# Flamingo attention with routed experts: key projection moved from 256-column to 512-column matmuls with dimensions on the partitions, rotary halves crossed by ScalarE, values of two head pairs in one product

## What is computed

```
lat = layer_norm(_layernorm(x));  ctx = layer_norm(context)
q = (lat @ Wq)                       # 16 heads of 64, "pairs" of heads are 128 columns
k, v = split(ctx @ Wkv)
k = apply_rope(k, cos, sin)          # x1*cos - x2*sin | x2*cos + x1*sin, halves of 32 in each head
attn = softmax(clip(q k^T / 8, -11, 11))
x = x + tanh(g_xattn) * ((attn @ v) @ Wo + bo)
x = x + tanh(g_ffn) * (routed experts + shared expert)(_layernorm(x))
```

## Time and profile before

| | |
|---|---|
| median of 3 runs | 2723.12 us |
| profiled execution, its own time | 2726.36 us |
| its span, first to last instruction | 2724.6 us |
| TensorE busy | 2419.1 us, 89% |
| VectorE busy | 2125.0 us, 78% |
| GpSimd busy | 1989.4 us, 73% |
| ScalarE busy | 1163.4 us, 43% |
| mean granted TensorE clock | 0.96 of full speed |

### The profile page before, as it was taken

One profiled execution on the slowest core, in us unless ns is written; L12 is line 12 of the kernel. 1 busy time (PEld: TensorE's weight loads), 2 busy tenths in 40 slices (PEclk: granted clock), 3 DMA queues, 4 the chain that ended last, 5 costly groups with the idle time before them and its releaser, 6 DMA issues. The chain is left out here.

```text
span 2724.6 us, 47912 instructions
## 1 busy us (share of the span) xinstructions
PE 2419.1 (89%) x13494; PEld 1471.9 (54%) x13494; DVE 2125.0 (78%) x4785; ACT 1163.4 (43%) x2652; POOL 1989.4 (73%) x2550
## 2 busy tenths in 40 slices
PE   2999999999989998999999899989996986998991
PEld 1555555555555555555555555545553655987780
DVE  4877788887888787878778787888787666688884
ACT  2444444444344444443444344344442332676660
POOL 2777677689868886988698789868885731067776
PEclk9999999999989998999899999999997997999995
DMA  8334334111111211111121111111111516799994
GB/s 302 136 123 147 109 109 148 47 45 49 49 46 48 69 47 45 49 51 54 40 67 50 48 45 49 49 46 50 68 47 53 198 38 239 238 309 318 328 324 148
DMA packets 157368, 301.61 MB, mean 111 GB/s; under 512 B 20066, under 2 KB 95778, under 8 KB 156834
## 3 DMA queue, kind: packets, MB, share of 16 engines
q1 hardware_dynamic: 128994, 230.95, 25.0%
q0 software_dynamic: 24576, 67.14, 7.5%
q10 hardware_dynamic: 3520, 0.27, 0.1%
HBM read 170.37 MB, written 127.93 MB: 109 GB/s over the span
## 5 line engine op out<-in xcount | busy, mean ns | idle before, releaser
L925 ACT ACTIVATE e<-scores 128x1024 f32<-128x1024 f32 x520 | 533.9, 1027 | 920.0 <-PE scores L807 897.3
L1020 POOL TENSOR_SCALAR e<-e 128x1024 f32<-128x1024 f32 x520 | 613.7, 1180 | 50.4 <-ACT e L925 6.9
L1200 DVE TENSOR_TENSOR e_sum<-e_sum,e 128x1024 f32<-128x1024 f32 x391 | 582.1, 1489 | 5.7 <-POOL e L1020 5.5
L847 PE MATMUL ps_o<-e,v 128*64 128x512 f32 x2088 | 567.5, 622 | 0.4 <-POOL e L1020 0.4
L807 PE MATMUL scores<-q_t,k_t 64*128 64x512 f32 x3120 | 503.8, 427 | 28.9 <-DVE affine L1143 13.9
L819 PE MATMUL ps_kv<-w,ctx_t 128*128 128x256 f32 x3072 | 507.7, 302 | 11.9 <-DVE ctx_t L1150 8.5
L819 PEld LDWEIGHTS ps_kv<-w,ctx_t 128*128 128x128 f32 x3072 | 401.4, 191 | 202.0 <-issue 173.5
L807 PEld LDWEIGHTS scores<-q_t,k_t 64*128 64x128 f32 x3120 | 257.5, 185 | 391.3 <-issue 251.5
L1728 POOL DMA_INDIRECT room<-results_in_blocks,index x256 | 247.0, 965 | 210.4 <-DMA results_in_blocks<-room 130.5
L1010 POOL TENSOR_TENSOR k_rot<-rope_c,rope_s 128x64 f32<-128x64 f32 x513 | 323.2, 630 | 68.4 <-PE ps_kt L837 23.0
L1014 POOL TENSOR_TENSOR k_rot<-rope_c,rope_s 128x64 f32<-128x64 f32 x513 | 203.6, 397 | 195.3 <-ACT e L925 193.0
(11 more groups left out here) (287 smaller groups left out, 3553.3 us busy)
## 6 DMA issues: line engine op xcount, KB each, us to landing
w<-w_pairs SPq DMA_DIRECT2D x65, 768.0 KB, 4.5
rows_in_blocks<-room SPq DMA_DIRECT2D x16, 2560.0 KB, 11.3
x_nat<-rows_in_blocks SPq DMA_DIRECT2D x160, 256.0 KB
results_in_blocks<-room SPq DMA_DIRECT2D x80, 512.0 KB
wo<-in_L_xattn_Wo SPq DMA_DIRECT2D x66, 128.0 KB, 4.5
x_nat<-in_ctx SPq DMA_DIRECT2D x64, 128.0 KB, 4.3
down_all<-in_L_ffn_down_w SPq DMA_DIRECT2D x16, 512.0 KB, 8.6
w_pairs<-w_split SPq DMA_DIRECT2D x8, 768.0 KB, 7.1
```

What stands on the lines that cost most here:

```text
L847: mm = pe.matmul(ps_o[hh * DH:(hh + 1) * DH, :], v[:, buf, tile, hh * DH:(hh + 1) * DH], e[:, tile % 4, hh * N:(hh + 1) * N], start=(tile ...
L925: act.activation(e[:, c % 4], scores[:, c % 2], ACT.Exp, scale=SCALE).then_inc(s_exp, 1)
L1020: pool.tensor_scalar(e[:, c % 4], e[:, c % 4], EXP_HI, EXP_LO, ALU.min, ALU.max).then_inc(s_clip, 1)
L1200: dve.tensor_tensor(total, e[:, 0] if c == 2 else total, e[:, tile % 4], ALU.add).then_inc(s_sum, 1)
```

## The change

Keys and values are projected apart. A "double" is two pairs. In the even pair of a double, each step projects the values of both pairs for 128 context rows (256 moving columns of `wv`, into `ps_v`); in the odd pair there is no such product. The keys of a pair are projected in two halves, at c = 0 and c = 4: the key columns of `wqk` are stationary and 512 context rows of `ctx_t` move, so that the result in `ps_k` has dimensions on the partitions and is not transposed. Queries move from c = 0 to c = 2 and use `ps_k` too.

The rotation of a half is a chain: ScalarE copies the four groups of 32 partitions crossed into `k_sw` (c = 0 and 4), VectorE multiplies `ps_k` by cos and `k_sw` by signed sin (c = 1 and 5), GpSimd adds the two (c = 2 and 6), ScalarE makes the high part (c = 3 and 7), VectorE the rest (c = 4 and 7). The product `o_n` is done in two halves (c = 3 before the clip, c = 4 behind it). In `boundary` the context comes before the latents. Slots and gates of the routing go to DRAM (`store_all`) and are read back in `finish_routing`, which frees SBUF for the cos and sin tables, now 128 x 1024, made in `setup` with 16 transposes.

```diff
-                    pe.wait_ge(s_rope, g * 8 + c + 1)
+                if project and jj == 0:
...
+                    pe.wait_ge(s_v, 1 + g // 2 * 8 + c)
...
-                            mm = pe.matmul(ps_kv[:, 0:2 * P], ctx_t[:, a, cc, c * P:(c + 1) * P],
-                                           w[:, jj, bb, cc, 1:3].rearrange("p t m -> p (t m)"),
+                            mm = pe.matmul(ps_v[:, 0:2 * P], ctx_t[:, a, cc, c * P:(c + 1) * P], wv[:, bb, cc],
...
+                if project and c in (0, 4):
...
+                    else:
+                        pe.wait_ge(s_qlo, 2 + g)
+                    pe.wait_ge(s_cos, 1 + g * 2 + half)
...
+                            mm = pe.matmul(ps_k[:], wqk[:, jj, bb, cc, 1], ctx_t[:, a, cc, half * N:(half + 1) * N],
...
-                if project or (attend and c < 2):
-                    pe.wait_ge(s_klo, 1 + g * 8 + c)
-                    pe.wait_ge(s_rot, 2 + g * 8 + c)
-                    pe.transpose(ps_kt[:, 0:P], k_rot[:, c % 2].rearrange("p h d -> p (h d)"), pers.ident[:]
-                                 ).then_inc(s_kt, 1)
...
+                if project and c in (0, 4):
+                    half = c // 4
+                    act.wait_ge(s_k, g * 2 + half + 1)
+                    act.wait_ge(s_turned, 1 + g * 2 + half)
+                    for q in range(4):
+                        to, of = slice(q * 32, (q + 1) * 32), slice((q ^ 1) * 32, (q ^ 1) * 32 + 32)
+                        st = act.activation(k_sw[to], ps_k[of], ACT.Copy)
+                    st.then_inc(s_swapped, 1)
...
+                if project and c in (3, 7):
+                    half = c // 4
+                    act.wait_ge(s_turned, 1 + g * 2 + half + 1)
+                    act.activation(k_t[:, jj, 0, half * N:(half + 1) * N], k_c[:], ACT.Copy).then_inc(s_khi, 1)
...
+                if project and c in (2, 6):
+                    half = c // 4
+                    pool.wait_ge(s_sin, g * 2 + half + 1)
+                    pool.tensor_tensor(k_c[:], k_c[:], k_sw[:], ALU.add).then_inc(s_turned, 1)
+                if c == 3:
+                    pool.wait_ge(s_rec, g * 2 + 1)
+                    pool.wait_ge(s_oraw, g + 1)
+                    pool.tensor_tensor(o_n[:, 0:D], o_raw[:, 0:D], r_den[:, 0:D], ALU.mult).then_inc(s_on, 1)
...
+                if project and c == 3:
+                    dve.wait_ge(s_qe, g + 1)
+                    dve.tensor_tensor(q_t[:, jj, 1], ps_k[:], f32(q_t[:, jj, 0]), ALU.subtract).then_inc(s_qlo, 1)
+                if project and c in (1, 5):
...
+                    dve.wait_ge(s_swapped, g * 2 + half + 1)
+                    dve.tensor_tensor(k_c[:], ps_k[:], rope.cos[:, tokens], ALU.mult).then_inc(s_cos, 1)
+                    dve.tensor_tensor(k_sw[:], k_sw[:], rope.sin[:, tokens], ALU.mult).then_inc(s_sin, 1)
```

More of the change, by code:

```diff
@@ L154, in part, with more_part, shaped @@
         assert self.taken_up <= ROOM
+        return self.shaped(a, shape)
+    def more_part(self, start, *shape):
+        n = math.prod(shape)
+        assert start + n <= MORE
+        return self.shaped(self.more[:, start:start + n], shape)
+    @staticmethod
+    def shaped(a, shape):
         if len(shape) == 2:
@@ L703, in batch @@
                 for p in range(PAIRS):
-                    pair(b, p // 2, p % 2, p)
+                    pair(b, p // 2, p % 4, p)
             if boundary:
                 boundary(0)
-            with eng.Fori(0, PAIRS // 2) as i:
-                for jj in range(2):
-                    pair(0, i, jj, None)
+            with eng.Fori(0, DOUBLES // 2) as i:
+                for m in range(4):
+                    pair(0, i * 2 + m // 2, m, None)
             batch(1)
@@ L1259, in _ @@
             sp.dma_start(sdn[:], ins["shared_down_w"].rearrange("(k p) n -> p k n", p=P)).then_inc(shared_loaded, 16)
+            for whole, dram in ((router.slot_all, slots_dram), (router.gate_all, gates_dram)):
+                sp.dma_start(whole[:, 0:last * GT].rearrange("p (g t) e -> p g (t e)", t=GT),
+                             dram.rearrange("g p n -> p g n")).then_inc(all_loaded, 16)
             for e in range(0, E_R, 8):
@@ L1537, in experts @@
         xs = pers.x_nat[:, 0:XR]
-        land = kept.part(TOP_K, D)
-        y = kept.part(YR, D)
+        land = kept.more_part(0, TOP_K, D)
+        y = kept.more_part(TOP_K * D, YR, D)
         x_t = pers.x_nat[:, XR:XR + 4]
@@ L1751, in program @@
         router = Router(nc, ctx, pers, kept)
-        setup(nc, pers, ins, w_dram)
-        attention(nc, pers, ins, w_dram, xs_dram, router)
+        with ExitStack() as tables:
+            rope = Rope(nc, tables)
+            setup(nc, pers, rope, ins, wqk_dram, wv_dram)
+            attention(nc, pers, rope, ins, wqk_dram, wv_dram, xs_dram, slots_dram, gates_dram, router)
+        kept.more = ctx.enter_context(nc.sbuf_tensor("more", [P, MORE], F32))
         up = ctx.enter_context(nc.sbuf_tensor("up_all", [P, E_R, D], F32))
-        finish_routing(nc, pers, ins, kept, router, up, xs_dram, table_dram)
+        finish_routing(nc, pers, ins, kept, router, up, xs_dram, table_dram, slots_dram, gates_dram)
         experts(nc, pers, ins, out, kept, up, xs_dram, y_dram)
```

347 lines of the change are left out of this document (197 added, 150 removed).

## The result

The changed kernel takes 2643.62 us (median of 4 runs, 2637.58 to 2649.16) against 2722.78 us for the kernel before on the same chip: a ratio of 0.9706, 95% interval 0.9682 to 0.973. It is faster by 79 us, where 155 were forecast.

A forecast was written before the change was run, and what follows sets the result against it. TensorE was taken to bound attention, with VectorE nearly as full in two pairs of eight. Terms: -102.8 - 32 - 61.2 + 38.5 + 2 = -155.5 us, from 2726.4 to 2570.9, as median 2568; range 2530 to 2635.

The forecast's parts named there:

- (a): TensorE in attention: 514 transposes of 0.20 us are gone, saving 102.8 us in full.
- (b): TensorE's projection: 6.06 us a pair instead of 6.56, through groups of 512 columns, saving 32 us.
- (c): TensorE's time by pair after the change: 29.3 us for an even pair, 22.7 for an odd one.
- the distances between queries: Sign in the timeline: queries of even pairs 29 to 32 us from the next, odd ones near 23.
- (d): TensorE's waits in attention: 23.4 us for `k_rot`, 30 for `o_n` and 7.8 for `ctx_t` go, together 61.2.
- (e): VectorE late in pairs 5 and 7: 5.5 us in each of 7 routed batches, +38.5 us, bounds 0 and 60.
- (f): ScalarE's crossed copies in the key chain: 0.59 us each, room for 1.5, so nothing charged.
- (g): GpSimd in attention: loses 16 rotary operations, gets two additions and `o_n` in halves, and gets easier.
- (h): Around attention: setup copies and transposes, routing read back in `finish_routing`, `wv` load: +2 us, bounds 0 and 8.
- pairs 1 and 3 over 24 us: Sign that the forecast of VectorE's lateness, +38.5 us, would be wrong.
- a granted clock below 1.00 in an odd pair: Sign that the whole forecast would be wrong; the clock fell before only around boundaries (0.89).
- Rival B: VectorE bounds all odd pairs through collisions with GpSimd, 42 us and some 35 more, about 2645 us; chance 20%.

The follow-up runs named there:

- f5: Kernel before plus three VectorE operations (128 x 512, two SBUF inputs) at c = 4 of pairs 5 and 7 of routed batches: attention ends 20.4 us later.
- f6: Kernel before plus three VectorE operations (128 x 512, two SBUF inputs) at c = 4 of pairs 2 and 4 of routed batches: attention ends 33.7 us later.
- e4: Changed kernel with one uncrossed ScalarE copy of 128 partitions for four crossed ones of 32: attention ends at 2024.3 us against 2018.6 for the changed kernel run again.
- e5: Changed kernel with the rotary additions moved from GpSimd to VectorE, right behind its products: 17 us gained against the changed kernel run again.
- e1: Changed kernel with GpSimd's clip cut to 8 of 1024 columns of each exponential: attention ends 97 us earlier.
- b1: Kernel before with GpSimd's clip cut to 8 of 1024 columns of each exponential: attention ends 90 us earlier.
- e3: Changed kernel with the rest of the queries ahead of the second reciprocal on VectorE: wait for it 44.4 to 15.0 us, no time gained.
- e7: Changed kernel with three pieces of VectorE's routing moved from odd pairs to the end of even ones: 25 us gained, 22 against the changed kernel run again.
- e2: Changed kernel with VectorE's reciprocals on half of the columns only: attention ends 25 us earlier, time by the ratio some 2628 us.
- f1: Changed kernel plus three VectorE operations (128 x 512, two SBUF inputs) at c = 4 of pairs 5 and 7 of routed batches: costs 28 us.
- f4: Changed kernel plus three VectorE operations (128 x 512, two SBUF inputs) at c = 4 of all eight pairs of the first batch: costs 7.9 us.

## Why the prediction was wrong

The direction was right, and the size was missed by the 8.6 us by which 2643.62 lies over the range, and by 76 us from the number. By the steps of the prediction:

- (a), 102.8 us: right. The transposes took 0.20 us each, and they are gone.
- (b), 32 us, is **the term that was mis-sized: it saved nothing**. With no transpose behind it the projection's distance is 0.91 in five of the eight steps of an even pair, and 0.82 only where keys or queries follow. A key group took 1.47 to 1.60, on average 1.53, where 1.39 was taken from queries that had a transpose behind them. So a pair has 4 x 0.87 + 2 x 1.53 = 6.56 us, which is what 8 x 0.82 took before. The queries, in no term, went from 1.39 to 1.53 as well, 9 us in 64 pairs. Where exactly the loss is booked is a choice: put the other way, a transpose that goes saves 0.11 us where the product moves up to the projection (0.82 + 0.20 less 0.91). Together (a) and (b) brought 3.2 us in two plain pairs, 104 in 32 doubles, and not 134.8.
  The formula that the prediction set aside stands in the Trainium skill (TensorE: Matmul & The Clock Gate, section Back-to-back issue gap) for a matmul by itself; the page says that in a stream with weight loads it is too low for few columns and too high for 512. The traces agree with the first, 137 to 152 ns for 256 columns against an estimate of 109 by the formula, and not with the second, 232 to 267 for 512 against an estimate of 216. That the formula would have had (b) at nothing, as it came, is luck.
- (c), an even pair of 29.3 and an odd one of 22.7 us: near. The stretches above hold one of the eight projections on the other side of the cut, 0.9 us, so 28.77 and 23.77 are 29.7 and 22.9, 0.5 more in two pairs; the pair of 28.09 from which it was worked out has 0.15 us of idle time in it. (The marker given for it, the distances between queries, was not right: queries at c = 2 cut the doubles elsewhere.)
- (d), 61.2: 60.5 measured.
- (e), 38.5, is **the step that failed**: the new waits for VectorE are some 96 us, beyond its upper bound of 60. VectorE's load was forecast well in pair 5 (25.9 us, 25.80 measured), and so were the waits for the queries in pairs 5 and 7 (half of 3.2 and all of 3.9, against 2.41 and 3.07). What failed is the rule that only a pair in which VectorE's busy time exceeds TensorE's loses time. The other pairs of a routed batch had 23 to 27 us of VectorE work in pairs of 24.7 to 33.6 us and lost it too: 0.6 each in pairs 1 and 3, and 3.3 a batch at the router's products (23.4 over seven batches), neither of which was in the sum; at the boundary 3.3 a batch, for which the sum had only what the 3.9 of pair 7 leave over 3.07. A stretch is tight by its latest result, not by its share, and f5 and f6 show that this held before as well: there a us of VectorE's work in pairs 2 and 4 cost 0.8 us, though it was busy for 25.3 and 23.6 of 32 us. A faster TensorE asks for every such result earlier.
- The price in (e), 0.62 for each of six operations, came from rows at a boundary, where GpSimd stands idle. In the loop the product with cos, with one input in PSUM, took 685 ns on average, the product with sin 767 and the rest of the keys 964, and `e_sum` went from 1.49 to 1.55: VectorE's busy time rose by 40 us, where -70 was forecast.
- (f) was right: 589 ns a copy, where 0.59 us was taken from the earlier trace rows, and e4 shows that nothing hangs on them. (g) GpSimd did get easier (73% to 68%), and with its additions moved (e5) the kernel gains more. (h): the last stages take 1.8 us less, not 2 more.
- The clock was in no term. It fell in pairs with long waits, to 0.95 in pair 2 and 0.94 in pair 5 of batch 4 (pair 5 had 1.00). By the key group of pair 5 that is 1.3 us a time. Worked out from the trace's clock records, TensorE lost 39 us of its busy time in attention to the lower clock before and 51 after.

In attention the terms add up to -157.5 us and -80.3 came, so 77 are missing, half of them in each of two places. TensorE's busy time fell by 96.8 us where (a) and (b) had 134.8: 38 short, of which 12 are the clock and the rest prices, (b) and the queries. Its idle time rose by 16.5 us where (d) and (e) had it fall by 22.7: 39 short. There (e) is 57 us out, and other waits that went and were in no term (`k_t` and `rope_s`, 9.9; one of 4.3 at the start of a boundary; short ones) hide a part of it. e1 and b1 bear out the first half: with the waits nearly equal the change is worth 87 us.

Two of the signs that the prediction gave for being wrong came up: pairs 1 and 3 over 24 us (24.72 and 25.88), and a granted clock below 1.00 in an odd pair.

Rival B came nearest in time (2645), by luck: it had VectorE bind all odd pairs through collisions, but plain odd pairs run at TensorE's pace, and half of what is missing is in TensorE's own work. Its mechanism has a part in the routed pairs, where most of the new waits go with the clips (e1). The collisions are there. GpSimd and VectorE at the same moment, pair 6 of batch 4:

```profile
1194.74 0.74 POOL L1108 TENSOR_TENSOR o_n<-o_raw,r_den 128x256 f32<-128x256 f32 x1
1195.56 3.54 POOL L1112 TENSOR_SCALAR e<-e 128x1024 f32<-128x1024 f32 x2
```

```profile
1194.78 1.78 DVE L1285 TENSOR_TENSOR e_sum<-e_sum,e 128x1024 f32<-128x1024 f32 x1 [0.31 <-POOL e L1112]
...
1198.13 2.05 DVE L1285 TENSOR_TENSOR e_sum<-e_sum,e 128x1024 f32<-128x1024 f32 x1
```

`e_sum` takes 1.78 and 2.05 us instead of some 1.21, and GpSimd's two clips 3.54 together where one alone takes 1.04: both sides pay. By the Trainium skill (SBUF — State Buffer, section Who interferes with whom) a VectorE instruction with two SBUF inputs contends with a GpSimd one that reads SBUF for an exclusive lock. The trace agrees; but by b1 and e1 the clips cost the kernel before nearly as much, 90 us against 97.

Open is how the 96 us split between VectorE's own work, its turns with GpSimd and the order of its queue. e1 shows that more than half of the waits for VectorE go with the clips, e3 that this change of order moves waits without gain, e7 that moving routing out of the tight pairs gains 25 us; no run here takes the routing away. The distances of (b) are read from the traces; why a group of 512 columns takes 1.47 to 1.60 us there and 1.39 before, no run isolates.

## What to carry to other kernels

When TensorE is made faster, list the results of the other engines that it waits for in each stage, and ask how early each can be ready; an engine that is busy for 80% of a stretch can have no room at all. Take the price of a group of matmuls from a row with the same group behind it: with another group behind them they came out 0.1 us dearer here, and that ate all of (b). To find out whether an engine has room costs one run before the change: add a few idle operations of a microsecond at the places in question, and see whether the end moves. When the named wait goes and the time stays (e3), the engine behind it is late as a whole, and what helped was to take work from it or from what it collides with (e2, e1), or to move work to another stretch (e7).

## What the runs showed of the hardware

- A copy on ScalarE from 32 partitions of PSUM to 32 others takes 589 ns for 512 columns, one of 128 partitions uncrossed 597 (e4): neither the number of partitions nor the crossing made it dearer.
- Six matmuls of 512 columns took 1.39 us up to a transpose behind them (queries, kernel before) and 1.47 to 1.60 up to a product with the values (keys and queries, changed kernel), at full clock without a wait. Six of 256 columns took 0.82 up to a transpose, keys or queries, and 0.91 up to that product.
- The same wait does not always cost the same clock: a wait of 2.41 us in pair 5 was followed by a key group of 2.93 us in two batches, and of 1.66 to 1.74 in four. A wait of 3.07 in pair 7 gave 2.88 once and 1.66 to 1.92 six times.
- The median length of an operation with two SBUF inputs, 128 x 512, was 0.68 us in f1 and 1.37 in f4 by its place beside GpSimd's clips, the shortest being 0.67 in both.
- In two sessions the kernel before took 2858.31 and 2869.26 us against 2722.78. In the changed kernel, run again in one of them, what follows attention took 769.2 us at 196 GB/s instead of 621.6 at 242, with attention ending at 2018.6. Whether it is the chip is not shown: the session of 2858.31 and a later one in which the kernel before took 2724.45 both bear the chip number 12.
